# Seven of eight MLP tiles a round turned by VectorE and four SBUF moves instead of by TensorE

## The reference

```python
k, v = ln(ctx) @ wk + bk, ln(ctx) @ wv + bv
slots = q_mu + exp(q_logsig) * layernorm(x)
for _ in range(3):
    q = ln(slots) @ wq + bq
    attn = softmax(einsum('bnd,bkd->bnk', k, q) / scale, -1) + 1e-8
    attn = attn / attn.sum(1)
    slots = einsum('bnk,bnd->bkd', attn, v) @ wu + bu + slots
    h = ln(slots) @ w1 + b1                  # the MLP: its input is what the change turns
    slots = gelu(h) @ w2 + b2 + slots
    slots = ln(slots + cond)
x = x + slots
x = x + routed_layer(layernorm(x))           # top 256 tokens: attention and a gated MLP
```

## Time and profile before

| | |
|---|---|
| median of three runs | 2311.74 us (2311.53 to 2314.35) |
| profiled execution | 2315.96 us, span 2314.3 us |
| busy TensorE, VectorE, ScalarE, GpSimd | 2275.8, 1501.0, 975.7, 1000.7 us |
| matmuls | 11317 |
| granted clock of TensorE, mean | 0.992 |
| packets of DMA, mean rate | 87122, 69 GB/s |

### The profile page before, as it was taken

The page is one execution under the profiler, slowest core; times in us unless marked ns, Lnnn a source line. Parts: engine busy times, 40 slices in busy tenths (PEclk is TensorE's granted clock), DMA queues, the critical chain, the costliest instruction groups (busy, mean ns, idle before and its releaser), DMA issues.

```text
span 2314.3 us, 30355 instructions
## 1 busy us (share of the span) xinstructions
PE 2275.8 (98%) x11317; PEld 1868.5 (81%) x11317; DVE 1501.0 (65%) x3056; ACT 975.7 (42%) x1650; POOL 1000.7 (43%) x1351
## 2 busy tenths in 40 slices
PE   8999999999999999999999999999999999999998
PEld 4788888888888888888888888888888887777886
DVE  6778557656476665769657576874766668764542
ACT  2566543343334333333333433333333345666432
POOL 3566235152453515435453452554535156653200
PEclk9999999999999999999999999999999999999999
DMA  5587000000152000013400001350000012204330
GB/s 202 181 315 283 3 1 1 1 1 1 37 208 79 1 23 5 15 50 128 155 6 21 8 10 55 113 170 5 10 19 1 21 55 81 74 29 146 97 113 19
DMA packets 87122, 158.54 MB, mean 69 GB/s; under 512 B 10801, under 2 KB 33337, under 8 KB 83134
## 3 DMA queue, kind: packets, MB, share of 16 engines
q1 hardware_dynamic: 82838, 150.26, 18.9%
q0 software_dynamic: 2688, 6.31, 0.9%
q10 hardware_dynamic: 1450, 0.04, 0.0%
HBM read 106.21 MB, written 50.37 MB: 68 GB/s over the span
## 4 chain that ended last, share of the span: by engine, by line
PE 81%; DVE 12%; POOL 2%; ACT 2%; issue 2%; DMA 0%; ACTq 0%; DVEq 0%; POOLq 0%
PE ps L218 25%; PE ps L220 25%; PE ps L219 25%; PE ps L1493 3%; DVE moments L1981 3%; DVE slots L2354 1%; DVE zTl L2029 1%; DVE tbuf L2341 1%; DVE tbuf L2348 1%; PE ps L444 1%; DVE mx L2303 1%; ACT prob L1885 1%; PE ps L1478 1%; PE ps L431 0%; PE ps L433 0%
## 5 line engine op out<-in xcount | busy, mean ns | idle before, releaser
L218 PE MATMUL ps<-zTh,kTl 128*128 128x512 f32 (+1 forms) x912 | 332.2, 364 | 2.9 <-ACT prob L1885 2.2
L220 PE MATMUL ps<-zTh,kTh 128*128 128x512 f32 (+1 forms) x912 | 324.6, 356 | 0.0
L219 PE MATMUL ps<-zTl,kTh 128*128 128x512 f32 (+1 forms) x912 | 324.3, 356 | 0.0
L218 PE MATMUL ps<-vh,prob_lo 128*128 128x512 f32 x768 | 304.6, 397 | 0.0
L220 PE MATMUL ps<-vh,prob_hi 128*128 128x512 f32 x768 | 299.9, 390 | 0.0
L219 PE MATMUL ps<-vl,prob_hi 128*128 128x512 f32 x768 | 299.2, 390 | 0.0
L2474 POOL TENSOR_SCALAR rs_m<-mv_m 128x1 f32<-128x1 f32 x96 | 60.2, 627 | 526.6 <-DVE mv_m L1983 526.6
L2029 DVE TENSOR_TENSOR zTl<-ps,zTh 128x512 fp32r<-128x512 f32 x224 | 151.0, 682 | 188.4 <-ACT zTh L1750 188.4
L1732 ACT ACTIVATE zbuf<-slots,rs_m 128x512 f32<-128x512 f32 x96 | 78.4, 816 | 333.7 <-POOL rs_m L2479 333.7
L1885 ACT ACTIVATE prob<-ps,nb 128x1024 f32<-128x1024 f32 x96 | 107.3, 1117 | 250.0 <-DVE nb L2308 246.0
L218 PEld LDWEIGHTS ps<-zTh,kTl 128*128 128x128 f32 x912 | 172.1, 189 | 35.1 <-DVE zTl L2029 7.1
(11 more groups left out here) (325 smaller groups left out, 5467.6 us busy)
## 6 DMA issues: line engine op xcount, KB each, us to landing
ctx<-in_ctx_dram SPq DMA_DIRECT2D x8, 1024.0 KB, 7.6
slots<-in_x_dram SPq DMA_DIRECT2D x8, 1024.0 KB, 6.7
kT_d<-kTh SPq DMA_DIRECT2D x6, 1024.0 KB, 8.1
kT_d<-kTl SPq DMA_DIRECT2D x6, 1024.0 KB, 10.6
s_d<-slots SPq DMA_DIRECT2D x6, 1024.0 KB, 5.2
v_d<-vh SPq DMA_DIRECT2D x6, 1024.0 KB, 9.2
v_d<-vl SPq DMA_DIRECT2D x6, 1024.0 KB, 11.2
kTh<-kT_d SPq DMA_DIRECT2D x3, 2048.0 KB, 11.0
```

The costliest lines, as they stand in the source:

```text
L218: nc.tensor.matmul(out, ll, rh, start=start, stop=False)
L219: nc.tensor.matmul(out, lh, rl, start=False, stop=False)
L220: return nc.tensor.matmul(out, lh, rh, start=False, stop=stop)
```

## The change

For tiles 0 to 6 of a round (`MOVED` = 7) TensorE's four transposes go. In their place VectorE turns the normalised tile in 32x32 blocks (`m_turn`): 16 blocks, each of every fourth column of one 128-column part, so that it reads `zbuf` with a stride of four floats. The result goes into the part of `prob` that update j has read (`blocks(j)`). SP then moves it with four DMAs from SBUF to SBUF (`move`), one for each group of 32 partitions, 64 KB each, 512 bytes for each piece, into another part of `prob` (`moved(j)`): the stride and the move together give partition p the model column p of each 128. ScalarE's `m_hi` and VectorE's `m_lo` read that instead of PSUM and wait for the move. Tile 7 is turned by TensorE as before. `m_normalize`, `m_hi` and `m_lo` stand about one update later in the orders of their engines, `m_hi(5)` and `m_hi(6)` between the GELUs, and VectorE's counts lie in other places among them. SP has the moves behind its other work of the round, with one `finish_out` behind move 4. Some semaphores are joined under other names (`nb_ready` into `mx_ready`, `bkv_shifted` into `consts`) with other counts and the same waits.

```diff
@@ -77,6 +77,19 @@
+    def blocks(j):
+        return prob[:, j // 4, 0:4, cut(j % 4)]
...
+    def moved(j):
+        return prob[:, j // 4, 4:8, cut(j % 4)]
...
+    MOVED = NT - 1
...
+    def moved_in(g, j):
+        n = MOVED * g + j
+        return f"moved_in{n % 2}", (n // 2 + 1) * 4 * 16
@@ -1386,6 +1399,15 @@
+            def move(g, j):
...
+                sp.wait_ge(sem("tr_m"), g * NT + j + 1)
+                done, n = moved_in(g, j)
+                if n > 4 * 16:
+                    sp.wait_ge(sem(done), n - 4 * 16)
+                for k in range(4):
+                    sp.dma_start(moved(j)[:, k, :], blocks(j)[cut(k, 32)]).then_inc(sem(done), 16)
@@ -1399,8 +1421,12 @@
                     if t < ROUNDS - 1:
-                        finish_in(b - 1, t, 2, g); finish_out(b - 1, t, 2)
+                        finish_in(b - 1, t, 2, g)
                 if t < ROUNDS - 1:
+                    for j in range(MOVED):
+                        move(g, j)
+                        if b and j == 4:
+                            finish_out(b - 1, t, 2)
                     continue
@@ -1657,8 +1687,8 @@
                     pe.wait_ge(sem("zo_m"), n8 + j + 1)
-                    if j >= 2:
-                        pe.wait_ge(sem("lo_m"), n8 + j - 1)
+                    pe.wait_ge(sem("lo_m"), n8 + j - 1)
+                    pe.wait_ge(sem("tr_m"), n8 + j)
                     transposes(zbuf[:, j % 2, :], 6 + j % 2).then_inc(sem("tr_m"), 1)
@@ -1691,13 +1721,12 @@
                 update(2)
-                m_transpose(0); update(3); m_transpose(1); update(4); m_transpose(2); update(5)
-                m_transpose(3); update(6); m_transpose(4)
+                update(3); update(4); update(5); update(6)
                 if g == 0:
...
                     hidden(0, f)
-                m_transpose(5); update(7); m_transpose(6)
+                update(7)
                 if g == 0:
@@ -1880,7 +1909,7 @@
                 for i in range(NT):
-                    act.wait_ge(sem("nb_ready"), n8 + i + 1)
+                    act.wait_ge(sem("mx_ready"), 3 * (n8 + i) + 3)
                     b0 = 2 * ((i + 1) % 3)
@@ -1906,7 +1935,13 @@
                 def m_hi(j):
-                    hi_transposed("m", n8 + j, j, j)
+                    if j == MOVED:
+                        hi_transposed("m", n8 + j, j, j)
+                        return
+                    done, n = moved_in(g, j)
+                    act.wait_ge(sem(done), n)
+                    A.activation(zT[0][:, :, cut(j)].rearrange("p c (a n) -> p c a n", a=4),
+                                 moved(j).rearrange("p a (c n) -> p c a n", c=C), ACT.Copy).then_inc(sem("hi_m"), 1)
@@ -1921,21 +1956,24 @@
                 prob_split_hi(g, 2); prob_split_hi(g, 3)
-                for j in range(2, 6):
-                    if j >= 4:
-                        prob_split_hi(g, j)
-                        m_hi(j - 4)
-                    m_normalize(j - 2)
-                    finishes(6 + j)
...
-                prob_split_hi(g, 6); m_hi(2); m_normalize(4)
-                prob_split_hi(g, 7); m_hi(3); m_normalize(5)
-                m_normalize(6); m_hi(4)
-                for f in range(C):
-                    gelu(0, f)
+                finishes(8)
+                prob_split_hi(g, 4); m_normalize(0); m_normalize(1)
+                finishes(9)
+                prob_split_hi(g, 5); m_hi(0); m_normalize(2)
+                finishes(10)
+                prob_split_hi(g, 6); m_hi(1); m_normalize(3)
+                finishes(11)
+                prob_split_hi(g, 7); m_hi(2); m_normalize(4)
+                m_hi(3); m_normalize(5)
+                m_hi(4)
+                gelu(0, 0)
+                m_normalize(6)
+                gelu(0, 1)
                 m_hi(5)
-                m_normalize(7); m_hi(6)
-                m_hi(7)
+                gelu(0, 2)
+                m_hi(6)
+                gelu(0, 3)
+                m_normalize(7); m_hi(7)
                 if last:
@@ -2301,12 +2339,12 @@
                     V.tensor_reduce(mx[:, i:i + 1], ps[:, b0:b0 + 2, :], AX.XY, ALU.max).then_inc(sem("mx_ready"), 1)
-                    dve.wait_ge(sem("mx_ready"), 2 * (n8 + i) + 1)
+                    dve.wait_ge(sem("mx_ready"), 3 * (n8 + i) + 1)
                     V.tensor_scalar(tm[:, i:i + 1], mx[:, i:i + 1], LOGIT_SCALE, cr[:, b, i:i + 1],
                                     ALU.mult, ALU.add).then_inc(sem("mx_ready"), 1)
-                    dve.wait_ge(sem("mx_ready"), 2 * (n8 + i) + 2)
+                    dve.wait_ge(sem("mx_ready"), 3 * (n8 + i) + 2)
                     V.tensor_scalar(nb[:, i:i + 1], cr[:, b, i:i + 1], tm[:, i:i + 1], None, ALU.subtract)\
-                        .then_inc(sem("nb_ready"), 1)
+                        .then_inc(sem("mx_ready"), 1)
                     if i >= EARLY:
@@ -2325,8 +2363,19 @@
+                def m_turn(j):
+                    dve.wait_ge(sem("zo_m"), n8 + j + 1)
+                    V.transpose(blocks(j), zbuf[:, j % 2, :].rearrange("p (c i g) -> p g c i", c=C, g=4)).then_inc(sem("tr_m"), 1)
...
                 def m_lo(j):
-                    lo_transposed("m", n8 + j, j, j)
+                    if j == MOVED:
+                        lo_transposed("m", n8 + j, j, j)
+                        return
+                    dve.wait_ge(sem("hi_m"), n8 + j + 1)
+                    V.tensor_tensor(zT[1][:, :, cut(j)].rearrange("p c (a n) -> p c a n", a=4),
+                                    moved(j).rearrange("p a (c n) -> p c a n", c=C),
+                                    zT[0][:, :, cut(j)].bitcast(f32).rearrange("p c (a n) -> p c a n", a=4),
+                                    ALU.subtract).then_inc(sem("lo_m"), 1)
@@ -2361,22 +2410,27 @@
                 add_update(1); finishes(9)
-                for j in range(4, NT - 1):
-                    add_update(j - 2); finishes(6 + j)
-                    split_prob(j)
-                    m_lo(j - 4)
+                split_prob(4); m_turn(0)
+                add_update(2); finishes(10)
+                m_turn(1); split_prob(5); m_lo(0)
+                add_update(3); finishes(11)
+                m_turn(2); split_prob(6); m_lo(1)
+                add_update(4); finishes(12)
+                m_turn(3); split_prob(7); m_lo(2)
                 add_update(5); finishes(13)
-                m_lo(3)
-                split_prob(7)
-                add_update(6); m_lo(4)
-                for j in range(4):
-                    count(j)
-                m_lo(5)
+                m_turn(4); m_lo(3)
+                add_update(6); m_turn(5); m_lo(4)
+                count(0)
+                m_turn(6)
                 if g == 0:
                     weight_lo(1)
-                count(4); count(5)
-                add_update(7); m_lo(6)
-                count(6)
+                count(1); count(2)
+                m_lo(5)
+                count(3)
+                m_lo(6)
+                count(4)
+                add_update(7)
+                count(5); count(6)
                 ranks = b and t == ROUNDS - 1
```

## The result

The changed kernel took 2277.03 us (2276.27 to 2277.97) against 2311.64 us, a ratio of 0.9848 with a 95% interval of 0.9831 to 0.9865. The forecast was 2274.5 with a range of 2268 to 2290. The gain of 37.4 us lies inside both intervals (31 to 39 us, and 36 to 42 us).

A forecast was written before the change was run, and what follows sets the result against it. TensorE, busy 98% of the span, was taken as the bound. Removing 84 tiles' transposes at 0.445 us takes 37.4 us off the 2311.74 us median, with turns and moves hidden: 2274.3, given as 2274.5, range 2268 to 2290.

The forecast's parts named there:

- The price of a tile: TensorE's stream: four transposes cost 0.445 us a tile; seven tiles in twelve rounds give 37.4 us.
- TensorE is not starved anywhere in the rounds: TensorE's waits: in the rounds only twelve of 0.2 us or less and 0.8 us once at a transpose.
- the hole of 0.8 us: A ranking round's end: TensorE busy 36.2 of 37.0 us, where VectorE is busy 35.7.
- Nobody becomes late: Before hidden(0, 0): VectorE has 1.85 us for each turn, 2.2 without finishing tiles, so 0.7 to 1.0 us is hidden.
- Nothing is added: VectorE's low halves, now reading SBUF in place of PSUM, take 0.6 us as before.
- The turn itself: VectorE's 32x32 block transpose with stride four: 0.7 to 1.0 us a tile, 2.76 us kept for the range.
- estimate of 1.24 us: VectorE's turn by the skill page: four 128x128 bf16 transposes at 311 ns; the sum 1.2 us more.
- Rival A: Ranking rounds' end: VectorE late above a turn of 1.05 us; 2277 at 1.4, 2284 at 2.0; chance 0.14.
- Rival B: Moves landing past 7.2 us delay tile 3: 2296 at 9 us, 2310 at 10.2 us; chance 0.07.
- each further microsecond is one in each round: Tile 3's move: past a landing of 7.2 us, each microsecond later adds one in each of twelve rounds.
- Rival C: At hidden(0, 0): strided turn over 2.6 us makes the kernel slower, 2320 at four passes, 2.76 us; chance 0.05.
- Rival D: TensorE keeps equal holes where the transposes stood, so removing them is free: 2312 us; chance 0.02.

The follow-up runs named there:

- one_of_four: The kernel before with one of the four TensorE transposes of tiles 0 to 6 kept, no turn or move; 2287.17 us, ratio 0.9889.
- order_only: The changed kernel's order without turn and move, TensorE transposing as before, tiles 5 and 6 between the hidden matmuls; 2314.32 us, ratio 1.0005.
- turn_x2: The changed kernel with every turn done twice on VectorE into the same place; 2341.61 us, ratio 1.0122.
- stride1: The changed kernel with the turn reading neighbouring columns instead of every fourth, so the output differs; turn 0.689 us, one execution 2275.8 us.
- late_tile3: The changed kernel with two more DMAs, each waited for, ahead of the four of tile 3's move; 2305.02 us, ratio 0.9959.
- late_more: The changed kernel with three more DMAs, each waited for, ahead of tile 3's move; 2350.18 us, ratio 1.0163.

## Why the prediction was right

*The price of a tile.* 84 x 0.445 = 37.4 us, read from the starts of the matmuls around a transpose, is near what a round shows (3.13 us for seven tiles), and `one_of_four` shows most of it (0.333 us a tile for three of four) with nothing else changed. The durations in the same row (0.60, or 4 x 0.27) would have given 50 or 91 us. At one and the same order a tile is worth 0.48 us (`order_only` against the changed kernel), 40 us in all; a cost of the new order that the prediction did not have, 0.2 us at down(4) in each of eight rounds, brought the sum back to it. That part of the fit is luck.

*TensorE is not starved anywhere in the rounds.* This reading of the waits was wrong. It missed the four waits for GpSimd (2.3 us) in the last rounds, and it put the hole of 0.8 us in a ranking round's end down to VectorE.

*Nobody becomes late.* Right, by less than was worked out. The prediction said four turns could take 1.85 us each before hidden(0, 0); with a turn of 1.07 the low half of tile 3 starts 1.3 to 2.4 us ahead of hidden(0, 0) in the twelve rounds. It ends 0.6 to 1.8 us ahead in eleven of them and 0.2 us ahead in round 0, where it took 1.75 us. Two terms of that sum were too small: low halves and splits that read SBUF are stretched beside GpSimd's work (up to 1.80 and 1.98 us), and a move takes 4.1 us, not 3.5, since an issue of a move takes 0.60 us and not 0.34. "Nothing is added" for the low half was wrong in 15 of 84 cases, and was hidden. `turn_x2` shows how much it matters: by the terms of rivals A and C 2289 was expected for a turn of 2.1 us, and it took 2341.6. Their limit of 2.6 us, from which the change would be slower than before, was too high: at 2.1 us the kernel is already 29 us slower than before.

*The turn itself.* 0.7 to 1.0 us taken, 1.07 measured, and `stride1` splits it into one pass of 0.69 and 0.385 for the stride. The Trainium skill (SBUF — State Buffer, "SBUF: two separate sides") says that an access to a new 16-byte line pays a penalty; the run agrees, 0.385 us for 512 such accesses, and it is far from the four passes of rival C. The estimate of 1.24 us that the prediction made from the Trainium skill's page VectorE: DVE Perf Modes ("The three transpose paths") is too high for this tile by 0.17 us; no run here turns a tile in bf16.

*Rival A, the ranking rounds.* The place was right, and the cause and the sign were not. With a turn of 1.07 the ranking rounds gained 3.83 us, 0.7 more than the others. The last round of element 0, where VectorE has no ranking, gained as much more (3.93). What goes there is TensorE's wait for GpSimd (1.01 to 0.54 us, and 0.69 to 0.24), and `order_only` shows the same without any turn. Three such excesses, 2.2 us, are nearly the difference between 37.4 and the 39.8 us between the two profiled spans; the text had them as a possibility below 2270 and counted none. Its sum for this rival is also loose by 0.3 us: from the level of 1.05 us that it names, a turn of 1.4 gives 2.1 us in three rounds and one of 2.0 gives 9.3 us in all, and its 2.4 and 9.6 go from a level of 1.0.

*Rival B, late moves.* Not here: 4.1 us, where the prediction allowed 7.2. The room was less than that: in `late_tile3` a landing at 8.2 us started hidden(0, 0) 1.9 us late, so that tile 3 has 6.3 us. The rate, "each further microsecond is one in each round", holds for a wait of 1.6 to 1.8 us (`late_tile3`) and not for one of 4 us (`late_more`: 5.6 to 7.3 us a round).

*Rival C* did not come, since the turn is 1.07 us. Its mechanism is the one that `turn_x2` then showed. *Rival D* is refuted: the holes closed.

What decides between slow steps and none in between stays open: of nine waits of 2.2 to 3.0 us in `turn_x2` and `late_tile3`, four had slow steps behind them (one of 2.26 us) and five had not (one of 2.98 us). Not followed up either is why GpSimd ends earlier in the last rounds with the new order.

## What to carry to other kernels

Price work on a pipelined TensorE by the starts of its instructions: what a group adds between the last matmul before it and the second behind it. If no wait of TensorE is in the rounds, that price comes off nearly whole, and it pays to give the engine with idle time more than twice the work (here 1.07 us of VectorE and four DMAs for 0.445 us of TensorE). Read the list of waits to its small lines before saying that there is none: a line of 2.3 us, left out here, decided how the rounds differ. Before taking more from the engine, find the next limit: here a wait for GpSimd and one for VectorE lay 0.2 us a round behind, and 0.45 to 1.3 us more a round out of TensorE bought nothing that could be told from the changed kernel.

## What the runs showed of the hardware

An idle TensorE can cost more than its idle time. Behind the waits of 3.7 us and more in `late_more` its granted clock fell to 0.50 (1.2 GHz) and 7 to 13 matmuls started 0.43 us apart in place of 0.227, in twelve of twelve places, for 1.7 to 2.8 us on top of each wait; behind the waits of 1.6 to 1.8 us in `late_tile3` never. A block transpose of 32x32 on 128x512 floats takes 0.689 us, and 1.07 us when it reads every fourth float. A VectorE subtraction of 128x512 with both sources in SBUF took 0.68 us alone and 1.28 us on average (up to 1.80) while GpSimd had a 128x512 operation under way; with one source in PSUM it stayed under 0.70 us beside such operations, 76 times of 76 in the kernel before. Four DMAs from SBUF to SBUF with 64 KB in pieces of 512 bytes, issued one behind the other, take SP 0.60 us each, a lone store of 256 KB 0.34 us, and the same store right behind them 0.59 us.
